# A third attention layer: keys kept as two F32R halves, scores in three products, GpSimd does the splitting

## The reference, cut to what matters

```
def _L2_xattn_ref(x, context, Wq, Wk, Wv, Wo, bo):
    q = (x @ Wq).reshape(b, n, h, d).transpose(0, 2, 1, 3)
    k = (context @ Wk).reshape(b, -1, h, d).transpose(0, 2, 1, 3)
    v = (context @ Wv).reshape(b, -1, h, d).transpose(0, 2, 1, 3)
    sim = jnp.einsum('bhid,bhjd->bhij', q, k) * scale
    attn = jax.nn.softmax(sim, axis=-1)
    out = jnp.einsum('bhij,bhjd->bhid', attn, v)
    return out.transpose(0, 2, 1, 3).reshape(b, n, h * d) @ Wo + bo
x = x + _L2_xattn_ref(_layernorm(x, axis=-1), ctx_768, ...)
```

## Time and profile before

| | |
|---|---|
| median of 3 runs | 2400.54 us |
| the profiled execution | 2401.57 us, its span 2399.7 us |
| busy over the span | PE 93%, PEld 80%, DVE 77%, ACT 62%, POOL 29% |
| chain that ended last | PE 75%, DVE 11%, ACT 6%, issue 5% |

### The profile page before, as it was taken

The page is one execution under the profiler, slowest core; times in us unless marked ns, Lnnn a source line. Parts: engine busy times, 40 slices in busy tenths (PEclk is TensorE's granted clock), DMA queues, the critical chain, the costliest instruction groups (busy, mean ns, idle before and its releaser), DMA issues.

```text
span 2399.7 us, 49297 instructions
## 1 busy us (share of the span) xinstructions
PE 2227.5 (93%) x14668; PEld 1913.3 (80%) x14669; DVE 1857.3 (77%) x4483; ACT 1493.9 (62%) x3090; POOL 686.7 (29%) x926
## 2 busy tenths in 40 slices
PE   7899999999899999995479999999998999989999
PEld 6788888888698788873257888888886788879998
DVE  3798888888876788887975887887888666866666
ACT  5566666666444677767886666666664655636666
POOL 2255555555412122210001111111102442422334
PEclk9999999999899999997589999999998999989999
DMA  8444454445201444430025445444442000114545
GB/s 216 118 141 129 142 146 142 131 138 147 69 0 37 125 132 126 138 111 16 0 67 152 135 134 152 138 145 140 140 132 62 1 1 2 38 54 141 140 140 158
DMA packets 461646, 256.58 MB, mean 107 GB/s; under 512 B 25664, under 2 KB 442332, under 8 KB 461532
## 3 DMA queue, kind: packets, MB, share of 16 engines
q1 hardware_dynamic: 461532, 255.27, 37.8%
HBM read 150.10 MB, written 105.12 MB: 106 GB/s over the span
## 4 chain that ended last, share of the span: by engine, by line
PE 75%; DVE 11%; ACT 6%; issue 5%; POOL 0%; ACTq 0%; DVEq 0%; POOLq 0%
PE ps_o L904 13%; PE ps_s L891 11%; PE ps_p L87 7%; PE ps_p L89 6%; PE ps_p L88 6%; PE ps_t L881 6%; PE ps_o L1474 3%; PE ps_t L1474 2%; PE ps_t L3129 2%; PE ps_s L3111 2%; PE ps_o L3129 2%; PE ps_s L87 2%; ACT a_keys L1022 2%; DVE a_sm L1197 2%; PE ps_s L89 2%
## 5 line engine op out<-in xcount | busy, mean ns | idle before, releaser
L904 PEld LDWEIGHTS ps_o<-a_val,a_pt 128*128 128x128 f32 (+2 forms) x3200 | 416.3, 193 | 34.9 <-issue 8.4
L904 PE MATMUL ps_o<-a_val,a_pt 128*128 128x128 f32 (+2 forms) x3200 | 426.6, 277 | 5.7 <-ACT a_pt L1059 3.6
L891 PE MATMUL ps_s<-a_keys,a_zt 128*128 128x308 f32 (+1 forms) x1024 | 414.3, 491 | 14.6 <-ACT a_keys L1022 9.8
L1031 ACT ACTIVATE a_stage<-ps_p 128x512 f32<-128x512 f32 (+1 forms) x370 | 221.2, 598 | 277.0 <-PE ps_p L89 275.5
L1197 DVE TENSOR_REDUCE a_sm<-a_e 128x16 f32<-128x1232 f32 (+1 forms) x192 | 234.3, 1220 | 179.4 <-ACT a_e L1067 178.9
L1059 ACT ACTIVATE a_pt<-ps_t 128x512 f32<-128x512 f32 (+1 forms) x448 | 225.1, 505 | 144.0 <-PE ps_t L881 142.7
L1022 ACT ACTIVATE a_keys<-ps_p 128x308 f32<-128x308 f32 x603 | 256.8, 427 | 79.5 <-PE ps_p L89 79.0
L87 PE MATMUL ps_p<-ct_hi,a_mt_hi 96*128 (+1 forms) x603 | 292.2, 485 | 0.0
L881 PE MATMUL ps_t<-ident,a_e 128*128 128x128 f32 (+1 forms) x1600 | 261.8, 276 | 25.1 <-POOL a_e L1214 13.6
L1067 ACT ACTIVATE a_e<-a_e 128x1232 f32<-128x1232 f32 (+1 forms) x192 | 203.9, 1062 | 52.8 <-DVE a_e L1189 36.4
L1214 POOL TENSOR_TENSOR a_e<-a_e,a_rs 128x539 f32<-128x539 f32 (+1 forms) x192 | 165.8, 891 | 231.3 <-DVE a_rs L1202 230.0
(11 more groups left out here) (437 smaller groups left out, 4939.4 us busy)
## 6 DMA issues: line engine op xcount, KB each, us to landing
a_vals<-a_stage SPq DMA_DIRECT2D x160, 512.0 KB, 3.5
a_val<-a_vals SPq DMA_DIRECT2D x128, 576.0 KB
f_w<-in_L_ffn_W_dram SPq DMA_DIRECT2D x129, 256.0 KB, 2.6
a_vals<-a_stage SPq DMA_DIRECT2D x40, 416.0 KB
a_val<-a_vals SPq DMA_DIRECT2D x64, 256.0 KB
a_val<-a_vals SPq DMA_DIRECT2D x128, 40.0 KB
x<-in_x_dram SPq DMA_DIRECT2D x8, 512.0 KB, 7.0
out_dram<-x SPq DMA_DIRECT2D x7, 512.0 KB, 6.7
```

The lines of the kernel that those rows point to most:

```text
L891: eng.matmul(c.ps_s[:, b, 0:nh * KEYS], zt, keys[:, h0:h0 + nh, :], start=True, stop=True)\
L904: mm = eng.matmul(c.ps_o[:, (i % 2) * P:(i % 2 + 1) * P], self.pt[0:r, n, :], self.val[0:r, i % 2, n, :], start=(n == 0), stop=(n == self. ...
L1031: eng.activation(self.stage[0:n, slot, BANK * (v % 2):BANK * (v % 2) + BANK], bank[0:n, :], ACT.Copy)\
```

## The change

In the third attention alone (`split=True`, and `in_place` because it has 16 heads):

- Keys and z are kept as a high and a low F32R half (`keys_hi`, `keys_lo`, `zt_hi`, `zt_lo`), and each score bank is three F32R products in place of one F32 product.
- There is one set of keys, not two: the 4 units of the next group that fit into what a tile's scores have just read are made behind those scores, into the same place. The layout alternates between two forms from group to group. The plan is 4 keys in every tile and (3,3,3,3,3,3,2,0) values.
- ACT copies a key unit to a ring of four (`unsplit`); POOL makes the high half (CAST) and the low half (subtract) of it. The first 16 key units are split by ACT and DVE, and z by ACT (two copies) and DVE (`split_zt`, once per group).
- The exponential of t+1 stands on ACT behind the second copy of the turned groups, not behind the third.
- The multiplication by the reciprocal is three instructions (7, 7 and 2 heads), each with its own signal to the group of transposes that reads it.
- The stage has two slots in place of five; in the first window e and pt lend three places.
- At the start 36 units stand before the first scores (43 before), and 8 more behind them.

```diff
-        self.zt = sb(ctx, n("zt"), [P, 2, GT * P], F32)
+        if split:
+            self.zt_hi = sb(ctx, n("zthi"), [P, 2, GT * P], F32R)
...
-        self.keys = sb(ctx, n("keys"), [P, 2, GT, H, KEYS], F32)
+            self.keys_hi, self.keys_lo = (sb(ctx, n("keys" + h), [P, 1 if self.in_place else 2, GT * H, KEYS], F32R)
+                                          for h in ("hi", "lo"))
+            self.zt_lo = sb(ctx, n("ztlo"), [P, 2, GT * P], F32R)
+            self.unsplit = sb(ctx, n("unsplit"), [P, self.RING, GT, KEYS], F32)
...
+        self.slots = 2 if self.in_place else self.STAGES
+            self.val_plan = (3, 3, 3, 3, 3, 3, 2, 0)
...
-        self.prob_parts = self.uses if self.masked else 1
+        self.prob_parts = self.uses if self.masked or split else 1
...
     def scores(self, eng, t, b, par, k, first=False):
+        if self.split:
+            mm = three_passes(eng, o, [z[:, par, cols] for z in (self.zt_hi, self.zt_lo)],
+                              [self.batch_of(keys, par, k, b) for keys in (self.keys_hi, self.keys_lo)])
...
+                        if k == 2 and self.split:
+                            eng.wait_ge(self.key_split.sem,
+                                        self.key_split.at(self.keys_for(w, par, b, last) + 1))
...
+    def keep_keys(self, eng, u, bank, n, slot):
+        eng.wait_ge(self.key_split.sem, self.key_split.at(n - self.RING + 1))
+        eng.wait_ge(self.proj_done.sem, self.proj_done.at(u + 1))
+        eng.activation(self.unsplit[:, slot, :, :], bank[:, 0:GCOLS].rearrange("p (b k) -> p b k", b=GT), ACT.Copy)\
+           .then_inc(self.proj_copied.sem, 1)
...
+                    if more and self.in_place and j == 1:
+                        self.exponentials(eng, t + 1, (k + 1) % 2)
...
-        eng.tensor_tensor(e, e, bc(self.rs[:, par, :], KEYS), ALU.mult).then_inc(self.probs_ready.sem, 1)
+        for heads in self.prob_heads():
+            eng.tensor_tensor(e[:, heads, :], e[:, heads, :], bc(self.rs[:, par, heads], KEYS), ALU.mult)\
+               .then_inc(self.probs_ready.sem, 1)
...
+    def split_keys(self, eng, u, n, par, h):
+        src = self.unsplit[:, n % self.RING, :, :]
+        hi, lo = self.unit_of(self.keys_hi, par, h), self.unit_of(self.keys_lo, par, h)
+        eng.wait_ge(self.proj_copied.sem, self.proj_copied.at(u + 1))
+        eng.tensor_copy(hi, src).then_inc(self.key_high.sem, 1)
+        eng.wait_ge(self.key_high.sem, self.key_high.at(n - (self.lead - self.vuses) + 1))
+        eng.tensor_tensor(lo, src, hi.bitcast(F32), ALU.subtract).then_inc(self.key_split.sem, 1)
...
+    def gpsimd_split(self, eng, v_last):
+        def window(w, more, last):
+            for i in range(self.WIN):
+                if more and i == self.WIN - 1:
+                    eng.wait_ge(self.proj_done.sem, self.proj_done.at(self.use(w, v_last) + 1))
+                    self.copy_window(eng, w + 2)
+                for kind, h, place in self.plan_of(i, last):
+                    if kind == "k":
+                        self.split_keys(eng, self.use(w, place), self.key_number(w, place, last),
+                                        self.key_group(i) % 2, h)
+                if i % GT == 2:
+                    self.ln.pool_bias(eng, g)
...
+                elif i % GT == 3 and g + 1 < GROUPS:
+                    self.ln.pool(eng, g + 1)
```

More of the change, by code:

```diff
@@ L723, in make_plan, with freed_by, make_plan_ahead @@
         return plan
+    def freed_by(self, k, par):
+        q = self.quads
+        if self.in_place and par == 0:
+            return [2 * k, 2 * k + 1, 2 * k + 8, 2 * k + 9]
+        return [q * k + j for j in range(q)]
+    def make_plan_ahead(self, last):
+        plan, place, v = [], 0, 0
+        for i in range(self.WIN):
+            keys = [("k", h) for h in self.freed_by((i + 2) % GT, self.key_group(i) % 2) if not last or i < 2]
+            values = [] if last else [("v", v + n) for n in range(self.val_plan[i])]
+            v += len(values)
+            units = values + keys if self.in_place else keys + values
+            plan.append([(kind, n, place + m) for m, (kind, n) in enumerate(units)])
+            place += len(units)
+        return plan
@@ new lines, in count_keys, with key_number, keys_for @@
+    @staticmethod
+    def count_keys(plan):
+        return sum(kind == "k" for mine in plan for kind, _, _ in mine)
+    def key_number(self, w, place, last=False):
+        plan = self.tail if last else self.plan
+        before = sum(kind == "k" and p < place for mine in plan for kind, _, p in mine)
+        return self.first - self.vuses + 2 * self.heads * w + before
+    def keys_for(self, w, par, b, last):
+        if not self.ahead:
+            head = sum(self.head_span(b)) - 1
+            for i in range(3) if par == 0 else range(3, 7):
+                for kind, h, place in self.plan_of(i, last):
+                    if kind == "k" and h == head:
+                        return self.key_number(w, place, last)
+            return self.key_number(w - 1, next(place for kind, h, place in self.plan[-1] if kind == "k" and h == head))
+        order = [h for k in range(GT) for h in self.freed_by(k, 1 - par)]
+        h0, nh = self.head_span(b)
+        return self.heads + 2 * self.heads * w + self.heads * par + max(map(order.index, range(h0, h0 + nh)))
@@ L958, in tensor @@
         eng.wait_ge(self.before.sem, self.before.at(1))
-        for u in range(self.first):
+        for u in range(self.lead):
             if u >= 5:
                 eng.wait_ge(self.proj_copied.sem, self.proj_copied.at(u - 4))
+                if self.split and u - 5 >= self.vuses:
+                    eng.wait_ge(self.key_split.sem, self.key_split.at(u - 5 - self.vuses + 1))
             if u < self.vuses:
@@ L1282, in body @@
                     self.shift(eng, t + 2, k % 2, found)
+                if self.split and k == 1 and not last:
+                    u = 1 + self.gcyc * g + 2 * self.uses
+                    self.split_zt(eng, g + 1, 1 - par, u)
                 self.residual(eng, t, k)
```

209 lines of the change are left out of this document (169 added, 40 removed).

## The result

| | before | after |
|---|---|---|
| median | 2404.74 us (20 runs, 2399.54 to 2407.06) | 2412.90 us (20 runs, 2407.41 to 2415.77) |
| ratio | | 1.0033, 95% interval 1.0026 to 1.0040 |
| the profiled execution | 2401.57 us | 2414.18 us, its span 2412.4 us |

The change makes the kernel slower by a third of a per cent, 8.2 us by the medians; 2393 was forecast, a gain. The 2412.90 lies at the upper end of the stated range. The two profiled executions differ by 12.6 us, because that of before lies 3.2 under its median and that of after 1.3 over. The third attention accounts for the 12.6: its first exponential starts at 1280.07 before and 1280.06 after, its last one 13.35 us later. The whole question is therefore the pace of the windows.

What follows compares the result with a forecast made beforehand. PE was taken to bound seven windows of the third attention. The windows' gain of -14.4, POOL's queue +3.5 and the ends +3 gave -7.9 us on 2401.57, forecast as a 2393 us median, range 2377 to 2413.

Steps and rivals of the forecast that it cites:

- Bound before: Third attention before the change: PE sets the pace of seven windows at 71.66 us; DVE bounds the last, 57.21 us.
- Term 1, the scores: Score products on PE: three F32R passes replace one F32 product, gaining 0.41 us a tile; PE's window becomes 68.4 us.
- the last rival: Score products on PE cost what they did, with passes of 0.26 us: window stays 71.7, time 2405 us; chance 0.05.
- Term 2, the size of the collisions: DVE's multiplication parts wait for POOL's instructions: w, this wait, is 0.85 us a tile, between 0 and 2.1.
- Term 2, the average: DVE and ACT's loop averages 8.70 us a tile, 69.6 a window; PE's 3 us lead makes only averages count.
- Term 2, `split_zt` "falls in a third tile and is covered": DVE's making of z's low half, some 0.65 us once per group, falls in a third tile and adds nothing.
- The exponential's place "beyond that I cost the move at nothing": Exponential moved on ACT: takes about 1 us from DVE's wait, letting the loop close at its own length; otherwise free.
- Parts, +0.16 a tile: DVE's multiplication in three instructions of 539, 539 and 154 columns takes 1.60 us, 0.16 more a tile.
- Term 3, POOL's queue: Splitting keys keeps POOL busy 64 of 69.6 us a window; late keys cost +3.5 us in all, 0 to +20.
- Term 4, the ends: Start, first window and last window of the third attention: fewer early key units against late units and collisions, together +3 us.
- The rival in which DVE and POOL hold each other up: Third attention: from w = 1.1 the loop exceeds 8.96 us a tile; 2419 us at 1.25, about 2412 at 1.15; chance 0.28.
- Light collisions: Third attention: parts fall where POOL waits, w at most 0.55; PE bounds windows at 68.4 to 68.5, 2380 us; chance 0.18.

Runs made afterwards that it cites:

- before_exp: The kernel before, with only the third attention's exponential moved behind the second copy of turned groups: 2404.41 us, ratio 1.0010.
- before_parts: The kernel before, with only the third attention's multiplication in three instructions with three signals: 2401.16 us, ratio 0.9992.
- part_act: The changed kernel with the multiplication in one instruction and the window copies on ACT instead of POOL: 2387.54 us, ratio 0.9940.
- part_act_f32: The changed kernel, multiplication in one instruction, window copies on ACT, each score bank one F32 product of the high halves: 2409.51 us, ratio 1.0024.
- exp_first: The changed kernel with the exponential behind the first copy of turned groups, multiplication still in parts: 2396.82 us, ratio 0.9977.
- exp_third: The changed kernel with the exponential behind the third copy of turned groups, multiplication still in parts: 2421.72 us, ratio 1.0083.
- one_part: The changed kernel with the multiplication in one instruction of 1232 columns, window copies still on POOL: 2393.78 us, ratio 0.9955.
- part_act_exp1: The changed kernel, multiplication in one instruction, window copies on ACT, exponential behind the first copy of turned groups: 2384.79 us, ratio 0.9931.

## Why the prediction was wrong, by its own steps

**Bound before.** Right: PE in seven windows. `before_exp` and `before_parts` did not move their pace.

**Term 1, the scores.** Right in the main. The passes of a score bank in after, on PE (start, us, as in the earlier trace rows):

```profile
1509.13 0.38 PE L87 MATMUL ps_s<-a_keyshi,a_zthi 128*128 128x462 f32 x1
1509.35 0.37 PE L88 MATMUL ps_s<-a_keyslo,a_zthi 128*128 128x462 f32 x1
1509.56 0.37 PE L89 MATMUL ps_s<-a_keyshi,a_ztlo 128*128 128x462 f32 x1
1509.77 0.30 PE L87 MATMUL ps_s<-a_keyshi,a_zthi 128*128 128x308 f32 x1
```

0.21 to 0.22 apart, 0.21 forecast. (That is 2.2 columns a ns, as for the passes of 308 and 512; at the granted clock of 1.00, 2.4 GHz, it is a tenth less than the "one column a cycle" of the last rival.) PE's window was to be 68.4; `part_act` has 69.06 busy, and F32 in its place costs 3.0 to 3.1 a window, 3.3 forecast. Of the 0.7 by which 69.06 exceeds 68.4, 0.4 is PE's other work in its new order, which had been put at nothing: `part_act_f32` has 72.04 where before had 71.67. The rival of unchanged products is out; its sum should have been 2407, since terms 3 and 4 are 6.5 and not 5.

**Term 2, the size of the collisions.** About right, as a mean. After in the third attention, by shape, the rows that answer to the earlier trace rows:

```profile
L1361 DVE TENSOR_TENSOR a_e<-a_e,a_rs 128x539 f32<-128x539 f32 x124 | 111.9, 943 | 2.1
...
L1361 DVE TENSOR_TENSOR a_e<-a_e,a_rs 128x154 f32<-128x154 f32 x62 | 33.3, 537 | 0.0
```

Against 720 (two) and 310 free that is 2 x 0.22 + 0.23 = 0.67 a tile, 0.85 forecast. The rule for one wait, the rest of POOL's instruction less 0.14, held: the first part in tile 0 began at 1501.85, when the copy from 1501.60 had 1.00 left, and by its single record took 1.59 us, 0.87 above its 0.72. The Trainium skill, SBUF — State Buffer, "Who interferes with whom", says that whichever of the two issues first blocks the other fully; the trace agrees but for the 0.14. Its case, a wait behind every part (1.9 a tile), appears in the middle windows in tile 0 (2.2) and nowhere else.

**Term 2, the average: the step that failed.** "PE has about 3 us of lead over DVE in a tile, so an average is what counts, not each tile." By that, the loop at this w was 8.5 and the window PE's 69. But the collisions weren't even. In tiles 3 to 6 they are 0 to 0.25, and PE, which has two or three value units there, sets the time; in tiles 7, 0, 1 and 2 they are 1.1, 2.2, 0.8 and 0.9, and DVE sets it. DVE can't carry its slack from the first four into the others, because the exponential stands on ACT behind copies of PE's turned groups of the tile before it: a tile that PE makes long makes the exponential late, by as much. PE can't carry its lead either, since two tiles of score banks are all it has. A window is then about a sum over tiles of the later of the two, and costs 72.9 where both averages are below 69.5 (PE's 69.06 in `part_act`, the loop's 8 x 8.5 = 68).

The two runs that move the exponential let one check this, as an estimate. DVE's tile without collisions is 7.60, with the layer norm's statistics (tile 1) 8.10 and with z (tile 2) 7.82, each from the distances above less the tile's collision; PE's tiles are those of `part_act`: 7.60, 8.82, 9.30, 8.86, 8.85, 8.88, 9.28 and 7.72 from tile 0 on. The collisions are each run's own, on average 0.72 a tile in after, 0.16 in `exp_first` and 0.98 in `exp_third`:

| a middle window | by the averages | sum of the later | measured |
|---|---|---|---|
| after | 69.3 | 72.6 | 72.9 |
| `exp_first` | 69.3 | 70.5 | 70.6 |
| `exp_third` | 70.6 | 72.4 | 73.9 |

The averages miss all three by 1.3 to 3.6. The sum comes within 0.3 in the first two, of which `exp_first` is the test, since after's own distances went into DVE's tiles. In `exp_third` it lacks 1.5, which is PE's wait for z's low half at the head of tile 3 (1.48, the longest of the row above). The table also says that the 25 us between the two runs are not the tie alone: moving the exponential changed the collisions too, and no run changes one without the other.

**Term 2, `split_zt` "falls in a third tile and is covered".** It is covered on DVE, but not for PE, whose first scores of the next group wait for it: 3.9 us in five waits over 1400 to 1800 us, 0.8 of the 2.5 that PE idles in a window. This wait appears where DVE arrives late; in `one_part` and `part_act` it is absent. No run takes it away by itself, so its share of the loss (some 5 us, as an estimate from six windows of 0.8) is not tested.

**The exponential's place "beyond that I cost the move at nothing".** Wrong in kind where POOL is loaded: the place also sets the phase of the multiplication against POOL (0.72 against 0.98 of collisions a tile) and how late z's low half is. The half of the move that the change made is worth the 8.8 us between `exp_third` and after; the other half, another 16.1, was left lying.

**Parts, +0.16 a tile.** True of their own length (1.58 against 1.44 in the traces; `before_parts` shows no loss), wrong as their price here. I had worked out that POOL's next instruction goes before the next part, and charged it to the collisions; I did not compare it with the one instruction, whose collisions I would have had to put at one wait. In `one_part` that comparison is 19.1 us.

**Term 3, POOL's queue.** +3.5 forecast, 0 found: PE never waits for key_split, and POOL is busy for 53.3 of 72.9 where I had 64; its two instructions for a unit take 1.39 on average, 0.16 above their free length, where I had let DVE hold each unit up by 0.3. Its rows of after, which answer to the earlier trace rows:

```profile
L1582 POOL TENSOR_TENSOR a_keyslo<-a_unsplit,a_keyshi 128x308 fp32r<-128x308 f32 x240 | 198.7, 828 | 19.2
L1580 POOL CAST a_keyshi<-a_unsplit 128x308 fp32r<-128x308 f32 x240 | 134.0, 558 | 130.2 <-ACT a_unsplit L1153 129.3
...
L1628 POOL CAST a_windowlo<-ct_lo 96x616 fp32r<-96x616 f32 x6 | 10.5, 1757 | 0.0
```

Where free they take 0.44 and 0.78 (0.44 and 0.84 forecast). What was late instead was the low half of the window copy, which I had placed but not followed to PE's first value unit: 0.4 us a window in after and 0.9 in `one_part`, where it was PE's largest wait for POOL:

```profile
PE ps_p L87 <- POOL a_windowlo L1628: 4.7, 5, 1.0
```

**Term 4, the ends.** +3 forecast, +5.4 found: the start 0, the first window +1.0, the last one +4.4, where tiles 0 to 3 collide (8.5, 9.5, 8.7 and 7.9 us; before 8.4, 7.5, 7.7 and 6.9).

**The sum.** -14.4 + 3.5 + 3 = -7.9 against +8.0 + 0 + 5.4 = +13.4 in the two profiles (+8.2 by the medians). The rival in which DVE and POOL hold each other up had the direction and nearly the time (2412 at w = 1.15), but not the way: w was 0.7, late keys were 0, and the slow tiles were five of eight, not all; so its nearness in time is luck. Light collisions, the rival at 2380, came true in kind in `exp_first`, `one_part` and `part_act`, for the reason it gave: in most tiles the multiplication falls when POOL has finished the last tile's units. Its numbers did not: windows of 69.3 to 70.6 where it had 68.4 to 68.5, and times of 2387.5 to 2396.8.

## What to carry to other kernels

Before averages of two engines are compared, ask for each tile which of them ends last and what ties them: an instruction on a third engine that waits for both (here the exponential, behind copies of PE's results) turns a mean with slack into a sum of maxima. Where two engines contend, cutting an instruction into parts gives the other one a seam to enter; leave it whole unless a reader waits for the first part. And look at where in its queue the shared instruction stands: here, with the parts, its place was worth 25 us between the earliest and the latest, about as much as the new product (22); with PE as the bound (`before_exp`, `part_act_exp1`) it was worth nothing that shows.

## What the runs showed of the hardware that was not expected

- The engine that comes second waits, whichever it is: POOL's subtraction of 0.79 us took 1.85 in `one_part`, where it starts (1490.32) inside the 1.70 us multiplication (from 1489.83).
- Not every POOL instruction holds DVE. The statistics' power over 128x4 takes 1.02 us, nearly as long as an add of 128x512 (1.28), and a multiplication that begins inside it takes its free 1.44 (`one_part`, POOL and the DVE row of 1497.55 above):

```profile
1497.41 1.02 POOL L304 TENSOR_TENSOR tail_rstd<-tail_var,neg_half 128x4 f32<-128x4 f32 x1
```

- ACT copies 96x616 with reordering in 1.30 us, POOL in 1.25 where free. In `part_act` PE never waits for the copy on ACT between 1400 and 1800 us:

```profile
L1308 ACT ACTIVATE a_windowhi<-ct_hi 96x616 fp32r x6 | 7.8, 1296 | 0.0
```
